# Single bias additions on GpSimd, wide conditioning products and a denser prologue in a two-layer conditioned attention kernel

## The chip, the cores and the metric

The kernel runs on one core of a Trainium2 chip. The metric is the device time of one execution in microseconds. TensorE (PE) does matrix products and transposes and writes to PSUM banks; VectorE (DVE), ScalarE (ACT) and GpSimd (POOL) work beside it; SyncE (SP) issues most DMA transfers from one queue, in order. Each engine runs its own instruction list in order and meets the others at semaphores.

## What is computed

Two attention layers, one behind the other, on x of shape (2, 1024, 256), float32, with a condition vector of 512 per batch element:

```
# layer 0: softmax attention, 16 heads of 16 channels
xn = layer_norm(x, norm_w, norm_b)
q, k, v = xn @ q_w + q_b, xn @ k_w + k_b, (xn @ v_w + v_b) * mask
att = softmax(q k^T + (1 - mask) * -1e6, over the keys)
y = att @ v
e = silu(emb) @ emb_w + emb_b              # (2, 512); scale, shift = its halves
h = layer_norm(y, sb_norm_w, sb_norm_b) * (1 + scale) + shift
x = x + silu(h) @ out_w + out_b
# layer 1: linear attention, 8 heads of 32 channels
q = softmax(xn @ Wq + bq, over channels); k = softmax(xn @ Wk + bk + mask term, over tokens)
v = (xn @ Wv + bv) * mask; y = q @ (k^T v); then as above with W_emb, b_emb, W_out, b_out
```

The condition's product e is small: 2 rows by 512 by 512 in each layer.

## The kernel before

Layer 0 is cut into 16 stages (`SUBS`): batch element x half of the queries (512) x group of 4 heads. A stage has 8 key tiles, so there are 128 steps (`STEPS`). In a step TensorE computes the scores of one key tile for four heads (`scores`, L969, four matmuls into the two double banks `sT`), ScalarE takes the exponential of both double banks (L803, `prob`), and in the next step TensorE multiplies with the values (`values`, L989, eight instructions into `acc`).

The softmax needs the largest score of each query before the exponential. So each stage has 32 "max" units (`MAXES`): TensorE computes scores with the queries as rows (L864) into one of three ring banks, VectorE reduces them (`halfmax`, L1162). The maxima of stage s+1 run beside the steps of stage s. Behind the last, VectorE makes `negmax` and splits it into two pieces (L1165, the cast L1168, L1170), TensorE transposes them (unit "neg", L882), VectorE copies them to `crows`, and SP loads them as rows of the queries (`load_max`). These small operations stand in VectorE's order behind maximum 32 and ahead of the maxima of the stage after.

All other work is cut into units placed beside the steps. A unit is filled by TensorE (`fill`) and taken out of its bank by ScalarE (if its kind is in `ON_ACT`) or VectorE:
- "rep" (L871, L875): queries and keys of group 0, replicated so that stage 0's maxima can start early.
- "qk" (L899): projection of queries and keys of one head group for 512 tokens; ScalarE writes its high part to `parts` (L735), VectorE the rest (L1203). `parts` has two buffers, group parity. `store_parts` writes them to HBM and `load_keys` and `load_queries` bring them back as stacked rows. Before ScalarE overwrites a buffer it waits for the stores of the group that held it.
- "v" (L839, L841): value projections of 256 tokens with a bias row `brow`; ScalarE writes `vp` (L746).
- "T" (L892): transposes of normalised rows `z`; "y", "neg", "kT", "qT": other transposes.
- "emb" (L913): e, as 4 x 4 products of a 128 x 128 weight block with two columns of the condition (`scond`), per layer; VectorE adds the bias (L1207), and behind the second computes the modulations.
- "out0", "keys", "queries", "values", "att", "y1", "out1": output projection of layer 0 and layer 1.

A planner writes `at[key]`, a spot of half a step, for each unit: `put` gives large kinds odd spots only, kinds in `SMALL` any. `places(k)` then says how many maxima stand at four places of step k (five where it has a large unit, three otherwise), and a rule on due times corrects the count. Before the steps runs a prologue: `pro_first`, then stage 0's 32 maxima with units of `between` among them (`pe_beside` is TensorE's order, `dve_beside` VectorE's), then `pro_last`. `warm` and `unread` issue matmuls of `ident` (L996) whose results nobody reads.

GpSimd normalises rows (`normalise`, L637 to L653) and adds output biases to `xs` (`add_bias`, L660): eight additions of 128 x 256 per batch element and layer. In layer 0 both elements' sixteen follow each other.

SP's list is: loads of inputs; `store_parts`, `load_keys`, `load_queries` of groups 1 and 2; the loads of `embw`, bias rows, `wo0` and `w1`; then per step the stores, loads and `load_max` that fall due.

Of the kernel before, what the change touches and what calls it, by code (L numbers as in the profile page):

```python
# [21 lines left out]
def two_layer_conditioned_attention(  # L22
# [59 lines left out]
    with ctx:  # L82
# [60 lines left out]
        def by_channel(flat):  # L143
            return flat.rearrange("p (k n) -> p k n", k=KC)
# [6 lines left out]
        qT = by_channel(late[:, 4 * TD:5 * TD])  # L151
        mrow = late[:, TD:TD + T]
# [53 lines left out]
        ON_ACT = {"T", "v", "values", "kT", "qT"}  # L206
# [5 lines left out]
        SMALL = {"T", "kT", "qT", "att", "vec2"}  # L212
# [33 lines left out]
        last = put([("qk", 0, 3, 0), ("qk", 0, 3, 1), ("qk", 0, 0, 1), ("v", 0, 3)], 0)  # L246
        last = put([("T", "in0", 1, h, kc) for h in range(NH) for kc in range(KC)], last)
        last = put([("emb", 0), ("emb", 1)], last)
        last = put([("qk", 1, hg, n) for hg in range(HG) for n in range(NH)], last)
# [109 lines left out]
        between = [("rep", *REPS[3]), ("qk", 0, 1, 0), ("rep", *REPS[4]), ("qk", 0, 1, 1), ("rep", *REPS[5])] + [("v", 0, i) for i in range(3)]  # L359
        pro_last = [("qk", 0, 2, n) for n in range(NH)]  # L360
        pe_beside, dve_beside = [], []
        for i in range(MAXES // 4):
            pe_beside += stream[4 * i:4 * i + 3] + [("warm", between[i], 1)] + stream[4 * i + 3:4 * i + 4] + [between[i]]
            behind = [between[i - 1]] if i > 0 and between[i - 1][0] != "v" else []
            dve_beside += stream[4 * i:4 * i + 2] + behind + stream[4 * i + 2:4 * i + 4]
        pe_beside += [("warm", pro_last[0], 2), ("neg", 0)] + pro_last
        dve_beside += [("neg", 0)] + pro_last
        pro_order = pro_first + between + pro_last
# [108 lines left out]
        def _(sp):  # L477
# [91 lines left out]
            for i, src in enumerate((emb_w, W_emb)):  # L569
                sp.dma_start(embw[:, i], src.rearrange("(e p) c -> p e c", p=P)).then_inc(embw_in, 16)  # L570
            for i, src in enumerate((out_b, b_out)):
                sp.dma_start(bias_rows[:, i, :], src.partition_broadcast(P)).then_inc(row_in, 16)
# [3 lines left out]
            for k in range(STEPS):  # L576
                for g in [3, 0] + list(range(HG, G)):
                    if k == begins["qk", g // HG, g % HG, 1] + 2:
                        store_parts(g)
                        if g == 3:  # L580
                            load_keys(g)
                s, c = where(k)
                if c == NT - 2 and s + 1 < SUBS:
                    load_max(sp, s + 1)
                if c == 0 and SLOTS <= s + 2 < SUBS:
                    load_queries(s + 2)
                if c == 0 and HG <= s - 1 < G:
                    load_keys(s - 1)
                if k == begins["emb", 1] + 2:
                    sp.wait_ge(emb_ready, 2)  # L590
                    load_mrow(0)
                if k == begins["att", 0, 1] + 2:
                    load_mrow(1)
                for half in range(2):
                    if k == begins["out1", 0, 2 * half + 1] + 2:
                        store(0, half)
# [5 lines left out]
        def _(pool):  # L602
# [52 lines left out]
            def add_bias(kind, b, row):  # L655

                for h in range(NH):
                    pool.wait_ge(z_ready[kind, b, h], QT)
                for t in range(b * NT, (b + 1) * NT):
                    pool.tensor_tensor(xs[:, t, :], xs[:, t, :], bias_rows[:, row, :], op=ALU.add).then_inc(biased, 1)  # L660
# [6 lines left out]

            for key in on_pool:
# [17 lines left out]
        def _(act):  # L686
# [11 lines left out]
            def take(key, ending=False):  # L698
# [44 lines left out]
                elif kind == "v":  # L743
# [4 lines left out]
                    last.then_inc(u.done, 1)  # L748
                elif kind == "values":
# [74 lines left out]
        def _(pe):  # L824
# [19 lines left out]
            def fill(key):  # L844
# [61 lines left out]
                elif kind == "emb":  # L906
                    l = key[1]
                    if l == 0:
                        pe.wait_ge(embw_in, 16 * 2)
                        pe.wait_ge(scond_ready, 1)  # L910
                    for oc in range(2 * KC):
                        for e in range(EC):
                            last = pe.matmul(o[:, oc * B:(oc + 1) * B], embw[:, l, e, oc * P:(oc + 1) * P], scond[:, :, e], start=(e == 0), stop=(e == EC - 1))  # L913
# [147 lines left out]
        def _(dve):  # L1061
# [61 lines left out]
            def take(key):  # L1123
# [81 lines left out]
                elif kind == "emb":  # L1205
                    l = key[1]
                    dve.scalar_tensor_tensor(out=emb[:, l], in0=o[:, 0:2 * KC * B].rearrange("p (o b) -> p o b", b=B), scalar=0.5, in1=by_col(f"emb_b{l}", 2 * KC),  # L1207
                                             op0=ALU.mult, op1=ALU.add).then_inc(u.done, 1)
# [77 lines left out]
            for key in pro_first:  # L1286
                if key[0] == "rep":
                    take(key)
            for key in dve_beside:
                take(key)  # L1290
                if key == ("max", 0, MAXES // 2):
                    dve.wait_ge(bhi_ready, 1)
                    dve.tensor_tensor(brow[32:33, :, :], braw[32:33, :, :], bhi[32:33, :, :], op=ALU.subtract).then_inc(brow_ready, 1)
# [30 lines left out]
```

## Time and profile before

| | us |
|---|---|
| median of three timed runs | 640.61 |
| lowest and highest of them | 638.69, 641.88 |
| the profiled execution | 630.65 |
| its span, first to last instruction | 628.7 |
| TensorE matmul busy | 580.3 (92%) |
| VectorE busy | 458.1 (73%) |
| ScalarE busy | 336.9 (54%) |
| GpSimd busy | 73.7 (12%) |

Matmuls overlap and their ends are modelled, so busy TensorE is not TensorE at its peak. The profile also records the clock granted to TensorE: 1.00 is 2.4 GHz, 0.50 is 1.2 GHz. Its mean over the span is 0.961. Times of rows count from the span's start.

### The profile page before, as it was taken

Reading aid. Unit: us, or ns where it says so; the run is one execution under the profiler, and the core shown is the slowest. Engines: PE = TensorE matmul, PEld = TensorE weight load, DVE = VectorE, ACT = ScalarE, POOL = GpSimd, SP = SyncE. Lnnn points to the kernel's source line nnn. Section 1 sums busy time; section 2 is a strip of 40 time slices with the busy share of each in tenths; the row PEclk is TensorE's granted clock in tenths of the full one; section 3 lists DMA queues with packets and bytes.
Section 4 is the critical chain, followed back from the end, with each engine's and each line's share of the span. In section 5 each row is a group of like instructions: output and inputs, shape, how many; then the busy total and the mean of one; then the engine's idle time right before and its main releaser. Section 6 shows DMA issues by size and latency. Waiting matters only on the chain.

```text
span 628.7 us, 8510 instructions
## 1 busy us (share of the span) xinstructions
PE 580.3 (92%) x3128; PEld 288.6 (46%) x3128; DVE 458.1 (73%) x916; ACT 336.9 (54%) x408; POOL 73.7 (12%) x125
## 2 busy tenths in 40 slices
PE   8999987999999999999998999999898999988986
PEld 7346335633453334344333434555334443524665
DVE  6585985378768899888889979868979897314543
ACT  2224461245558875646776655474574656771531
POOL 3000271000000040100002050000052001002200
PEclk9899996599999999999999979999989999999898
DMA  5245883127521003210330100010001100000001
GB/s 130 75 100 107 201 299 82 34 52 175 134 68 28 27 14 66 56 25 1 79 79 2 26 1 27 0 27 35 27 0 55 41 2 0 2 0 1 0 2 67
DMA packets 18579, 33.74 MB, mean 54 GB/s; under 512 B 3930, under 2 KB 10450, under 8 KB 17772
## 3 DMA queue, kind: packets, MB, share of 16 engines
q1 hardware_dynamic: 18412, 33.17, 21.2%
q8 instruction: 25, 0.41, 0.3%
q14 instruction: 14, 0.11, 0.1%
q10 hardware_dynamic: 128, 0.04, 0.0%
HBM read 19.29 MB, written 13.52 MB: 52 GB/s over the span
## 4 chain that ended last, share of the span: by engine, by line
PE 69%; DVE 22%; ACT 5%; issue 2%; DMA 1%; POOL 1%; SPq 0%; ACTq 0%; DVEq 0%; POOLq 0%
PE bank L989 16%; PE bank L864 13%; DVE halfmax L1162 12%; PE bank L839 8%; PE sT L969 7%; PE sT L839 3%; PE sT L864 3%; PE bank L899 3%; DVE stats L1076 2%; PE bank L913 2%; PE bank L925 2%; ACT hT L728 2%; ACT prob L803 2%; PE sT L871 2%; PE bank L996 2%
## 5 line engine op out<-in xcount | busy, mean ns | idle before, releaser
L803 ACT ACTIVATE prob<-sT 128x1024 f32<-128x1024 f32 x256 | 247.7, 1023 | 141.8 <-PE sT L969 141.5
L1162 DVE TENSOR_REDUCE halfmax<-bank 128x1 f32<-128x512 f32 x420 | 265.8, 683 | 54.6 <-PE bank L864 52.7
L864 PE MATMUL bank<-ks,qs 50*128 50x512 f32 x420 | 157.3, 483 | 17.4 <-DVE halfmax L1162 9.2
L989 PE MATMUL bank<-prob,vp 128*17 128x512 f32 x1024 | 139.7, 618 | 0.6 <-ACT prob L803 0.6
L864 PEld LDWEIGHTS bank<-ks,qs 50*128 50x128 f32 x420 | 64.5, 188 | 127.6 <-DVE halfmax L1162 76.1
L969 PE MATMUL sT<-qs,ks 52*128 52x512 f32 x512 | 108.2, 430 | 3.7 <-ACT prob L803 1.6
L637 POOL TENSOR_TENSOR rstd<-var,neghalf 128x4 f32<-128x4 f32 x14 | 14.2, 1015 | 532.1 <-DVE var L1086 532.1
L1162 DVE TENSOR_REDUCE halfmax<-sT 128x1 f32<-128x512 f32 x92 | 59.4, 685 | 11.6 <-PE sT L864 10.4
L969 PEld LDWEIGHTS sT<-qs,ks 52*128 52x128 f32 x512 | 54.8, 191 | 20.2 <-ACT prob L803 11.1
L839 PE MATMUL bank<-w,hT 128*128 128x256 f32 x152 | 38.7, 388 | 1.2 <-ACT hT L728 1.2
L989 PEld LDWEIGHTS bank<-prob,vp 128*17 128x17 f32 x1024 | 17.1, 96 | 40.6 <-issue 37.6
L839 PEld LDWEIGHTS bank<-w,hT 128*128 128x128 f32 x152 | 26.5, 189 | 9.0 <-issue 4.8
L864 PEld LDWEIGHTS sT<-ks,qs 50*128 50x128 f32 x92 | 8.8, 187 | 41.5 <-ACT prob L803 41.5
L864 PE MATMUL sT<-ks,qs 50*128 50x512 f32 x92 | 23.5, 508 | 0.5 <-ACT prob L803 0.5
L660 POOL TENSOR_TENSOR xs<-xs,bias_rows 128x256 f32<-128x256 f32 x32 | 22.0, 731 | 1.7 <-DVE z L1103 1.6
L899 PE MATMUL bank<-hT,wqk 128*128 128x512 f32 x44 | 21.6, 614 | 0.1
L735 ACT ACTIVATE late<-bank,cols 128x512 fp32r<-128x512 f32 x11 | 7.6, 689 | 26.2 <-PE bank L899 26.2
L892 PE MATMUL bank<-ident,z 128*128 128x128 f32 x96 | 14.7, 283 | 4.4 <-DVE z L1103 2.3
L1182 DVE RECIPROCAL rden<-bank 128x16 f32<-128x16 f32 x16 | 4.0, 251 | 20.1 <-PE bank L887 20.1
L841 PE MATMUL bank<-brow,ones 128*128 128x256 f32 x36 | 16.8, 468 | 0.0
L925 PE MATMUL bank<-hT,w 128*128 128x512 f32 x28 | 15.6, 682 | 1.1 <-ACT hT L728 1.1
L728 ACT ACTIVATE hT<-bank,modB,modA 128x512 f32<-128x512 f32 x12 | 9.1, 777 | 13.5 <-PE bank L892 13.1
(166 smaller groups left out, 559.1 us busy)
## 6 DMA issues: line engine op xcount, KB each, us to landing
stack_rows<-late SPq DMA_DIRECT2D x12, 512.0 KB, 6.0
qs<-stack_rows SPq DMA_DIRECT2D x30, 192.0 KB, 3.4
ks<-stack_rows SPq DMA_DIRECT2D x14, 384.0 KB
stack_rows<-late SPq DMA_DIRECT2D x17, 256.0 KB, 5.3
out_x<-xs SPq DMA_DIRECT2D x4, 512.0 KB, 3.0
xs<-in_x SPq DMA_DIRECT2D x4, 256.0 KB, 3.8
xs<-in_x SPq DMA_DIRECT2D x2, 512.0 KB, 4.2
late<-in_L_cond_emb_w SPq DMA_DIRECT2D x1, 1024.0 KB, 9.4
```

The costliest lines, as they stand in the source:

```text
L660: pool.tensor_tensor(xs[:, t, :], xs[:, t, :], bias_rows[:, row, :], op=ALU.add).then_inc(biased, 1)
L728: act.activation(hT[:, kc, h * HALF:(h + 1) * HALF], u.bank, func, scale=scale, bias=bias).then_inc(u.done, 1)
L803: act.activation(prob[:, c % 2, 2 * u:2 * u + 2, :].rearrange("p j n -> p (j n)"), sT[u][:, :], ACT.Exp).then_inc(exp_done, 1)
L839: last = pe.matmul(o[:, i * D:(i + 1) * D], hT[:, kc, tokens], w[:, kc, :], start=(kc == 0), stop=(kc == KC - 1 and row is None))
L841: last = pe.matmul(o[:, i * D:(i + 1) * D], ones[:, :], brow[:, row, :], start=False, stop=True)
L864: last = pe.matmul(o, qs[rows, s % SLOTS, c, t * P:(t + 1) * P], ks[rows, hg, c, half * HALF:(half + 1) * HALF], start=True, stop=True)
L892: last = pe.transpose(o[:, i * P:(i + 1) * P], z[:, h * QT + i, kc * P:(kc + 1) * P], ident[:, :])
L899: last = pe.matmul(o, wqk[:, kc, hg, :], hT[:, kc, n * HALF:(n + 1) * HALF], start=(kc == 0), stop=(kc == KC - 1))
L925: last = pe.matmul(o, w1[:, 1, k, kc * P:(kc + 1) * P], hT[:, k, n * HALF:(n + 1) * HALF], start=(k == 0), stop=(k == KC - 1))
L969: last = pe.matmul(sT[u][:, two * HALF:(two + 1) * HALF], ks[rows, hg, u, c * P:(c + 1) * P], qs[rows, s % SLOTS, u, :], start=True, stop= ...
L989: last = pe.matmul(acc[32 * j:32 * j + VW, :], vp[:, b, c, hg * GH + j, :], prob[:, c % 2, 2 * u + two, :], start=(c == 0), stop=(c == NT ...
L1162: dve.tensor_reduce(halfmax[:, s % 2, r, half:half + 1], o, axis=AX.X, op=ALU.max, negate=True).then_inc(u.done, 1)
```

## The change

Five edits:
1. `add_bias`: each addition on GpSimd first waits until the one before is complete.
2. "emb": the condition's two columns are the stationary operand and the 512 weight columns stream past, four products per layer into two rows of a bank. ScalarE copies them, halved, to `erow`. A new small unit "embT" transposes them by four 2 x 128 transposes, and VectorE adds the bias. "embT" stands behind the first two projections of batch element 1.
3. The prologue puts a unit behind every three maxima, without `warm` matmuls between, and has ten such units instead of eight: group 2's two projections have moved in among them. Each unit's part on VectorE comes after the second maximum of the next three.
4. Group 3's projections close the prologue (`pro_last`) instead of standing in steps 0 and 1; group 0's second projection and the last value unit move up from steps 2 and 3 to 0 and 1, and steps 2 and 3 have no unit. SP stores and loads group 3 behind the load of `embw`.
5. The subtraction for `brow` moves from VectorE to the head of GpSimd's list behind its fills.

```diff
-        ON_ACT = {"T", "v", "values", "kT", "qT"}
+        ON_ACT = {"T", "v", "values", "kT", "qT", "emb"}
-        SMALL = {"T", "kT", "qT", "att", "vec2"}
+        SMALL = {"T", "kT", "qT", "att", "embT", "vec2"}
-        last = put([("qk", 0, 3, 0), ("qk", 0, 3, 1), ("qk", 0, 0, 1), ("v", 0, 3)], 0)
-        last = put([("T", "in0", 1, h, kc) for h in range(NH) for kc in range(KC)], last)
+        last = put([("qk", 0, 0, 1), ("v", 0, 3)], 0)
+        last = put([("T", "in0", 1, h, kc) for h in range(NH) for kc in range(KC)], max(last, 4))
         last = put([("emb", 0), ("emb", 1)], last)
-        last = put([("qk", 1, hg, n) for hg in range(HG) for n in range(NH)], last)
+        last = put([("qk", 1, 0, n) for n in range(NH)], last)
+        last = put([("embT", 0), ("embT", 1)], last)
+        last = put([("qk", 1, hg, n) for hg in range(1, HG) for n in range(NH)], last)
...
-        between = [("rep", *REPS[3]), ("qk", 0, 1, 0), ("rep", *REPS[4]), ("qk", 0, 1, 1), ("rep", *REPS[5])] + [("v", 0, i) for i in range(3)]
-        pro_last = [("qk", 0, 2, n) for n in range(NH)]
+        between = [("rep", *REPS[3]), ("qk", 0, 1, 0), ("rep", *REPS[4]), ("qk", 0, 1, 1), ("rep", *REPS[5])] + [("v", 0, i) for i in range(2)]
+        between += [("qk", 0, 2, 0), ("v", 0, 2), ("qk", 0, 2, 1)]
+        pro_last = [("qk", 0, 3, n) for n in range(NH)]
         pe_beside, dve_beside = [], []
-        for i in range(MAXES // 4):
-            pe_beside += stream[4 * i:4 * i + 3] + [("warm", between[i], 1)] + stream[4 * i + 3:4 * i + 4] + [between[i]]
-            behind = [between[i - 1]] if i > 0 and between[i - 1][0] != "v" else []
-            dve_beside += stream[4 * i:4 * i + 2] + behind + stream[4 * i + 2:4 * i + 4]
+        by_three = [stream[i:min(i + 3, MAXES)] for i in range(0, MAXES, 3)]
+        for three, key, former in zip(by_three, between + [None], [("rep", *REPS[2])] + between):
+            pe_beside += three + ([key] if key is not None else [])
+            dve_beside += three[:2] + ([former] if former[0] != "v" else []) + three[2:]
...
                 sp.dma_start(embw[:, i], src.rearrange("(e p) c -> p e c", p=P)).then_inc(embw_in, 16)
+            store_parts(3)
+            load_keys(3)
...
                 for t in range(b * NT, (b + 1) * NT):
+                    pool.wait_ge(biased, t + row * B * NT)
                     pool.tensor_tensor(xs[:, t, :], xs[:, t, :], bias_rows[:, row, :], op=ALU.add).then_inc(biased, 1)
...
+            pool.wait_ge(bhi_ready, 1)
+            pool.wait_ge(zero_ready, 1)
+            pool.tensor_tensor(brow[32:33, :, :], braw[32:33, :, :], bhi[32:33, :, :], op=ALU.subtract).then_inc(brow_ready, 1)
...
+                elif kind == "emb":
+                    act.activation(erow[:, key[1], :], u.bank[0:B, :], ACT.Copy, scale=0.5).then_inc(u.done, 1)
...
+                    for e in range(EC):
+                        last = pe.matmul(o[0:B, :], scond[:, :, e], embw[:, l, e, :], start=(e == 0), stop=(e == EC - 1))
+                elif kind == "embT":
+                    l = key[1]
+                    done = unit["emb", l]
+                    pe.wait_ge(done.done, done.done_at)
                     for oc in range(2 * KC):
-                        for e in range(EC):
-                            last = pe.matmul(o[:, oc * B:(oc + 1) * B], embw[:, l, e, oc * P:(oc + 1) * P], scond[:, :, e], start=(e == 0), stop=(e == EC - 1))
+                        last = pe.transpose(o[:, oc * B:(oc + 1) * B], erow[:, l, oc * P:(oc + 1) * P], ident[0:B, 0:B])
```

## Rows read from the trace of the kernel before

**Rows 1.** The page: TensorE's granted clock in 40 slices, and the chain of waits.
```profile
PEclk9899996599999999999999979999989999999898
PE 69%; DVE 22%; ACT 5%; issue 2%; DMA 1%; POOL 1%; SPq 0%; ACTq 0%; DVEq 0%; POOLq 0%
```

**Rows 2.** Windows: stretch, its length, busy us (instructions) per engine, clock, DMA share, GB/s.
```profile
19.85:26.69 6.84, 5.60 (x12) 2.02 (x11) 3.14 (x5) 0.78 (x1) 0.00 (x0) 0.75 0.45 155
...
53.99:60.09 6.10, 5.94 (x32) 3.85 (x31) 1.78 (x3) 3.42 (x5) 0.00 (x0) 1.00 0.06 12
60.09:80.83 20.74, 18.64 (x86) 8.01 (x86) 18.57 (x40) 10.67 (x15) 3.42 (x6) 1.00 0.90 218
...
90.89:98.94 8.05, 2.55 (x18) 0.95 (x17) 8.02 (x5) 2.45 (x3) 6.45 (x10) 0.94 0.73 150
98.94:121.79 22.85, 22.85 (x100) 17.04 (x100) 7.33 (x13) 4.47 (x5) 0.00 (x0) 0.50 0.07 19
121.79:128.20 6.41, 6.41 (x28) 2.57 (x27) 4.69 (x16) 1.94 (x2) 0.00 (x0) 0.73 0.26 82
133.23:138.26 5.03, 4.73 (x24) 1.67 (x23) 3.92 (x6) 2.60 (x3) 0.00 (x0) 1.00 0.20 44
160.72:166.16 5.44, 5.14 (x28) 2.07 (x27) 4.51 (x8) 2.60 (x3) 0.00 (x0) 1.00 0.95 215
166.16:171.44 5.28, 4.97 (x30) 2.74 (x29) 3.92 (x6) 2.61 (x3) 0.00 (x0) 1.00 0.36 84
186.76:189.39 2.63, 2.60 (x19) 0.90 (x17) 2.12 (x4) 2.44 (x4) 0.00 (x0) 1.00 0.00 0
...
222.06:225.90 3.84, 3.26 (x19) 1.22 (x19) 3.60 (x10) 1.94 (x2) 3.02 (x6) 1.00 0.01 2
```

**Rows 3.** GpSimd and VectorE on the timeline; then cpieces' durations in ns (min/median/max).
```profile
86.33 11.01 POOL L660 TENSOR_TENSOR xs<-xs,bias_rows 128x256 f32<-128x256 f32 x16
90.65 6.72 DVE L1168 CAST cpieces<-negmax 128x16 fp32r<-128x16 f32 x1
...
L1168 DVE CAST cpieces<-negmax x16: 174/175/6720, 53.5 to 532.7; 128x16 fp32r<-128x16 f32 x16
```

**Rows 4.** TensorE on the timeline: value matmuls, idle time, an emb unit; weight loads.
```profile
91.88 1.05 PE L989 MATMUL bank<-prob,vp 128*17 128x512 f32 x8
98.24 0.40 PE L882 MATMUL bank<-ident,cpieces 128*32 128x128 f32 x1 [5.30 <-DVE halfmax L1162]
...
112.31 1.91 PE L989 MATMUL bank<-prob,vp 128*17 128x512 f32 x8
...
114.87 6.98 PE L913 MATMUL bank<-scond,late 128*128 128x2 f32 x32
...
7.74 2.98 PEld L996 LDWEIGHTS bank<-ident 128*128 128x128 f32 x26
```

**Rows 5.** The prologue on the timeline: TensorE between maxima, and four maxima on VectorE.
```profile
34.35 0.73 PE L864 MATMUL bank<-ks,qs 50*128 50x512 f32 x3
35.02 0.49 PE L996 MATMUL sT<-ident 128*128 128x128 f32 x2
36.06 1.98 PE L899 MATMUL sT<-hT,wqk 128*128 128x512 f32 x4
37.98 0.73 PE L864 MATMUL bank<-ks,qs 50*128 50x512 f32 x3
...
42.02 1.41 PE L864 MATMUL bank<-ks,qs 50*128 50x512 f32 x3
...
46.89 2.48 DVE L1162 TENSOR_REDUCE halfmax<-bank 128x1 f32<-128x512 f32 x4 [0.96 <-PE bank L864]
```

**Rows 6.** Timeline: VectorE's subtraction into brow; SP's first store and key load of group 2.
```profile
39.23 0.95 DVE L1293 TENSOR_TENSOR brow<-late 1x768 fp32r<-1x768 f32 x1
...
59.75 0.47 SPq L525 DMA_DIRECT2D stack_rows<-late  x1
...
68.58 0.78 SPq L534 DMA_DIRECT2D ks<-stack_rows  x2
```

More of the change, by code:

```diff
@@ L151, in two_layer_conditioned_attention @@
         qT = by_channel(late[:, 4 * TD:5 * TD])
+        erow = late[0:B, 4 * TD:4 * TD + 2 * E].rearrange("p (l c) -> p l c", l=2)
         mrow = late[:, TD:TD + T]
@@ L358, in two_layer_conditioned_attention @@
         pro_first += [("T", "in0", 0, 1, kc) for kc in range(KC)] + [("rep", *REPS[2])]
-        between = [("rep", *REPS[3]), ("qk", 0, 1, 0), ("rep", *REPS[4]), ("qk", 0, 1, 1), ("rep", *REPS[5])] + [("v", 0, i) for i in range(3)]
-        pro_last = [("qk", 0, 2, n) for n in range(NH)]
+        between = [("rep", *REPS[3]), ("qk", 0, 1, 0), ("rep", *REPS[4]), ("qk", 0, 1, 1), ("rep", *REPS[5])] + [("v", 0, i) for i in range(2)]
+        between += [("qk", 0, 2, 0), ("v", 0, 2), ("qk", 0, 2, 1)]
+        pro_last = [("qk", 0, 3, n) for n in range(NH)]
         pe_beside, dve_beside = [], []
-        for i in range(MAXES // 4):
-            pe_beside += stream[4 * i:4 * i + 3] + [("warm", between[i], 1)] + stream[4 * i + 3:4 * i + 4] + [between[i]]
-            behind = [between[i - 1]] if i > 0 and between[i - 1][0] != "v" else []
-            dve_beside += stream[4 * i:4 * i + 2] + behind + stream[4 * i + 2:4 * i + 4]
+        by_three = [stream[i:min(i + 3, MAXES)] for i in range(0, MAXES, 3)]
+        for three, key, former in zip(by_three, between + [None], [("rep", *REPS[2])] + between):
+            pe_beside += three + ([key] if key is not None else [])
+            dve_beside += three[:2] + ([former] if former[0] != "v" else []) + three[2:]
         pe_beside += [("warm", pro_last[0], 2), ("neg", 0)] + pro_last
         dve_beside += [("neg", 0)] + pro_last
+        assert len(by_three) == len(between) + 1
         pro_order = pro_first + between + pro_last
@@ L576, in _ @@
             for k in range(STEPS):
-                for g in [3, 0] + list(range(HG, G)):
+                for g in [0] + list(range(HG, G)):
                     if k == begins["qk", g // HG, g % HG, 1] + 2:
                         store_parts(g)
-                        if g == 3:
-                            load_keys(g)
                 s, c = where(k)
@@ L588, in _ @@
                     load_keys(s - 1)
-                if k == begins["emb", 1] + 2:
+                if k == begins["embT", 1] + 2:
                     sp.wait_ge(emb_ready, 2)
@@ L1204, in take @@
                                              op0=ALU.add, op1=ALU.subtract).then_inc(u.done, 1)
-                elif kind == "emb":
+                elif kind == "embT":
                     l = key[1]
-                    dve.scalar_tensor_tensor(out=emb[:, l], in0=o[:, 0:2 * KC * B].rearrange("p (o b) -> p o b", b=B), scalar=0.5, in1=by_col(f"emb_b{l}", 2 * KC),
-                                             op0=ALU.mult, op1=ALU.add).then_inc(u.done, 1)
+                    dve.tensor_tensor(emb[:, l], o[:, 0:2 * KC * B].rearrange("p (o b) -> p o b", b=B), by_col(f"emb_b{l}", 2 * KC), op=ALU.add).then_inc(u.done, 1)
                     dve.wait_ge(u.done, u.done_at)
@@ L1285, in _ @@
             dve.wait_ge(rep_cols_ready, 1)
-            for key in pro_first:
-                if key[0] == "rep":
-                    take(key)
+            for i in range(2):
+                take(("rep", *REPS[i]))
             for key in dve_beside:
                 take(key)
-                if key == ("max", 0, MAXES // 2):
-                    dve.wait_ge(bhi_ready, 1)
-                    dve.tensor_tensor(brow[32:33, :, :], braw[32:33, :, :], bhi[32:33, :, :], op=ALU.subtract).then_inc(brow_ready, 1)
             for k in range(STEPS + 2):
```

## Prediction

> **What bounds the kernel now.** I read the page first. The chain of waits is 69% TensorE and 22% VectorE, so the kernel lives on TensorE's sequence with VectorE close behind. The row of granted clocks has one deep notch, slices 7 and 8 of 40 (94 to 126 us), and a shallow one in slice 2 [rows 1]. The whole change lies ahead of 190 us, so I cut that stretch: TensorE's score matmuls (L969, four instructions per step) give the start of each of the 128 steps, and the view by windows, asked at those starts, gives one row per step or stage [rows 2]. The reader should compare steps that hold the same work. A step with one projection unit takes 5.03 us (the row 133.23:138.26), with a "y" unit beside it 5.44, with a value unit 5.28, a step with three maxima and a small unit 2.63. Against that step 6, also three maxima and a small unit, took 8.05, and steps 7 and 8, with the two "emb" units, took 22.85 together at clock 0.50. Step 9 took 6.41.
>
> What lies between is on the timeline [rows 3]. GpSimd runs 16 bias additions as one train from 86.33 to 97.34 us. VectorE's little cast (L1168) starts at 90.65 inside it and ends at 97.37, the moment the train ends: 6.72 us where the median of 16 is 175 ns. It is queued ahead of the maxima, which free the banks, so TensorE stands idle for 5.30 us. Right behind that the granted clock drops from 2.4 to 1.2 GHz: the same eight value matmuls take 1.91 us that elsewhere take 1.05, and an "emb" unit's 32 narrow products take 6.98 us [rows 4]. One collision thus pays twice.
>
> **The change part by part.** The sum is against the profiled execution: 628.7 us of span, 630.65 us in all, which is 10.0 us below the median of the three timed runs, 640.61.
>
> *Additions one by one.* Each of 32 additions waits for the former's completion. Nothing but later GpSimd work is queued behind them, and the first reader of a biased row is an output projection 35 steps later, so their lengthening is free. The cast then finds a gap, after at most one addition: a train of 11.01 us for 16 gives 0.69 each [rows 3]. Step 6 becomes 2.63 to 3.3 us; I take 2.8. Gain 5.2.
> The Trainium skill ("SBUF — State Buffer", section "SBUF: two separate sides") says that GpSimd and a two-port VectorE instruction take the shared port pair exclusively, for one whole instruction. By that rule the old cast should have lost one addition, 0.7 us; the trace disagrees, since it lost ten. Were the rule all there is, single additions would change nothing and the stall would need another cause; that is rival B.
>
> *Wide conditioning products.* Per layer 16 products of 2 columns (32 instructions) become 4 products of 512 columns, which at two instructions each, like L899's, are 8. Then comes one ScalarE copy and, later, four tiny transposes ("embT"). At full clock a projection of 4 such instructions costs 1.92 us (36.06 to 37.98) at about 0.43 each [rows 5], so 8 cost 3.64. The 32 narrow ones cannot be seen at full clock; nearest are the 26 weight loads of L996, 2.98 us, 0.115 each [rows 4], so 3.7. At equal clock the new form is worth nothing. At the clock of before it was 6.98. The bounds on what it is worth are therefore 0 and 2 x 3.3 us, and this depends on the clock. With TensorE no longer standing idle at 93 us I expect 2.4 GHz here, so steps 7 and 8 cost 5.03 + 1.72 = 6.75 each, 13.5 instead of 22.85: gain 9.35. Step 9, at full clock, is like step 17: 5.44 instead of 6.41, gain 1.0. ScalarE's copy falls into its idle time, since it is busy for only 2.60 us of a projection step's 5.03 [rows 2].
> "embT" makes a step of its own, step 11, and pushes ten later units one step back, to step 23, which was free. So the unit is not lost, but two small units are added: eight 0.115 us at most plus waits, 0.3 to 1.2 us; I take a loss of 0.6. VectorE's modulations move with it; they are needed only by "mid0", from step 34.
>
> *The prologue in threes.* Before, the first 32 maxima ran in eight fours, with a unit behind each four. From three maxima to the next three, a projection group took 3.63 (34.35 to 37.98), a replication group 4.04 (to 42.02), and in each of them 1.04 us (35.02 to 36.06) were the idle-filling matmuls (L996) and the fourth maximum, which waited for its bank [rows 5]. Now there are ten groups of three and a rest of two, without L996. By subtraction a group costs 2.59 and 3.00; one with a value unit 2.84, since a value step is 0.25 longer than a projection step [rows 2]. VectorE takes 0.62 per maximum (four in 2.48 [rows 5]) and for the unit about as much, 2.5 in all, so it hides, barely. The ten units are three replications, four projections and three values: 9.0 + 10.4 + 8.5 = 27.9 us. The first group starts at 19.85 as before, so the last unit ends at 47.7. Then the last two maxima must still be reduced (2 x 0.62) and followed by three small operations (0.2 each with their gaps), 2.0 us, which before ran beside the last value unit. From there the two final projections, L996 and step 0 follow as before, about 5.8 of the 6.10 us of the row 53.99:60.09: 55.5 us instead of 60.09 for the start of step 0, 4.6 earlier. The first group of before contained clock 0.75 on average and 1.24 us of waiting; whether that low stretch stays is open (0 to 1.5 us of loss), so I take a gain of 4.0, range 2.5 to 6. The subtraction into brow (0.95 us on VectorE [rows 6]) goes to GpSimd, idle then: 768 elements at 0.69 us per 256 are 2.1 us. By the group costs, ScalarE's two copies behind the third unit are done at about 30.5, GpSimd at 32.6, and the first value unit asks at 19.85 + 3 x 3.00 + 2 x 2.59 + 0.65 = 34.7: covered by 2 us.
>
> *The fourth group's projections ahead.* The two projections of group 3 leave steps 0 and 1. Steps 0 and 1 now hold what steps 2 and 3 held, and steps 2 and 3 hold no unit; the planner gives them 4 and 6 maxima. Step 36, five maxima and no unit, took 3.84, so I take 3.2 and 4.45. With 4.2 for step 0, which has no value matmuls but a small unit (5.03 - 1.05 + 0.2), and 5.28 for step 1 that is 17.1 instead of 20.74 [rows 2]: gain 3.6. The price on the queues: storing and loading of group 3 (four stores, two loads) now stand on SP's queue ahead of the bias rows, the output weights and layer 1's weights, whose first reader, GpSimd's additions, has slack. The additions may even start behind the cast now. Group 0's second projection comes at step 0 instead of 2, and ScalarE, before it writes its buffer, waits for group 2's stores. Those took from 59.75 until about 68.5 us [rows 6], 8.8 us, though issued only once group 2 is done. Now they would be issued at about 50.5 and land at 59.3; ScalarE asks at about 59.5. Cover nil, cost 0 to 1.5 us, in the range.
>
> Sum: 5.2 + 9.35 + 1.0 - 0.6 + 4.0 + 3.6 = 22.55 us, so 608.1 us for an execution like the profiled one and 618.1 if the 10.0 us to the median stay. Part of these 10 us can hardly be anything but longer stretches of low clock, and the largest such stretch goes away; I forecast 616.
>
> **Rivals.**
> A, *the clock falls elsewhere*. All the gain of steps 7 to 9 is clock. Steps 2 to 5 are now filled by VectorE's maxima (up to six per step), TensorE has gaps there, and idle TensorE is what preceded both notches. A stretch as long as the old one (steps 7 to 9, 29.3 us for what is worth 18.9) costs 10.4: 628.5. Against it: full clock held through steps 4 and 5, which have the same six maxima.
> B, *the train is not broken*. GpSimd takes the next addition so soon that the cast still waits for all, or the stall had another cause. Then step 6, the clock and steps 7 to 9 stay as before, wide products included, since 8 at half clock cost 7: gain 4.0 + 3.6 - 0.6 = 7.0, 633.6.
> C, *slower: the clock in the prologue*. The matmuls without use between the maxima are gone, and if the clock falls at 23 us, as it did before [rows 1, 2], it may not come back. TensorE's work from 19.85 to step 0 is some 30 us at full clock; at half it is up to 30 us more. Against a gain of 22.5 this decides from three quarters of the stretch at low clock: 640 to 648. Against it: groups with 2.5 of 2.6 us busy are busier than before.
> D, *a queue*. Group 2's stores land late and ScalarE holds up exponentials and maxima, or the first value unit waits for brow: 5 to 20 us, 621 to 638.
>
> **How the numbers follow.** Forecast 0.70, A 0.17, B 0.05, C 0.03, D 0.05. The likeliest case gives 616; its own spread is 603 (26 us gained and none of the 10 us left) to 624, and the range goes on through A to 630. A measurement can tell 0.5%, 3.2 us, from no change. Faster by more holds in the forecast, A, B and most of D, 0.94; within 0.5% the rest of D and a little of C, 0.03; slower 0.03.
>
> **What would show it.** Right: no cast above 1 us; no idle of TensorE above 1.5 us between 75 and 100 us; granted clock 1.0 in steps 6 to 9; the emb products 16 instructions at about 0.43 us from one to the next; step 0 at 54 to 57 us; steps 2 and 3 together under 8.5 us; step 10 starting 20 to 25 us earlier than 128.20. Wrong: a low clock of over 10 us anywhere ahead of 130 us (A or C), a cast of several us (B), ScalarE idle behind group 2's stores in step 0 (D).

## The result, and the profile after

The changed kernel takes 616.06 us (median of four runs, 610.35 to 622.21) where the kernel before takes 639.65 in the same comparison; the ratio is 0.965, 95% interval 0.959 to 0.971. The forecast was 616. The four runs lie in two pairs, 610.35 and 612.59 at mean clocks of 0.979 and 0.985, and 619.52 and 622.21, slow ones, at 0.958 and 0.960, so that no single run took 616. Measured again later beside the kernel before (e12) the ratio was 0.972, 0.967 to 0.976. The profiled execution took 610.35 us with a span of 608.5 us, 20.3 us less than the profiled one of before; the sum had said 22.55.

The page of the changed kernel, TensorE's share and its granted clock, beside [rows 1]:

```profile
PE 564.3 (93%) x3072; PEld 273.3 (45%) x3072; DVE 450.8 (74%) x915; ACT 337.9 (56%) x410; POOL 76.5 (13%) x126
...
PEclk9999899999999996999999999999899999999998
```

The notch in slices 7 and 8 is gone. A new narrow one (231 to 242 us) lies far behind the change, where the kernel before has one at 364 to 371 us, and a shallow one lies in slice 5.

The view by windows of the changed kernel at its own step starts (columns as in [rows 2]). In order: the ten groups of the prologue; from the last two maxima to step 0; steps 0 to 3; step 6; steps 7 and 8; step 9; steps 10 to 23.

```profile
19.92:48.47 28.55, 28.43 (x92) 13.77 (x91) 23.46 (x37) 9.26 (x15) 1.81 (x1) 1.00 0.56 132
48.47:58.44 9.97, 6.79 (x34) 4.25 (x33) 4.08 (x9) 3.24 (x4) 0.00 (x0) 1.00 0.57 131
58.44:77.93 19.49, 16.88 (x79) 7.51 (x80) 16.12 (x36) 9.35 (x12) 3.39 (x6) 0.91 0.94 252
88.41:90.60 2.19, 2.19 (x18) 0.83 (x17) 2.19 (x4) 2.05 (x3) 2.03 (x3) 1.00 1.11 357
90.60:102.77 12.17, 12.17 (x53) 3.12 (x52) 6.91 (x12) 5.33 (x7) 8.82 (x13) 1.00 0.21 61
102.77:107.65 4.88, 4.88 (x28) 2.05 (x27) 3.76 (x7) 2.53 (x3) 0.00 (x0) 1.00 0.00 0
107.65:171.16 63.51, 61.09 (x319) 26.63 (x320) 49.34 (x92) 35.51 (x44) 0.00 (x0) 1.00 0.50 121
```

Read against [rows 2]: step 6 took 8.05 and now 2.19; steps 7 and 8 took 22.85 at clock 0.50 and now 12.17 at 1.00; step 9 took 6.41 and now 4.88. These are 18.1 of the 20.6 us by which step 10 starts earlier (107.65 instead of 128.20). The prologue gave 1.65 (step 0 at 58.44 instead of 60.09) and steps 0 to 3 gave 1.25 (19.49 instead of 20.74). Steps 4 and 5 took 0.4 us more (10.48 instead of 10.06, each from the start of step 4 to that of step 6). Behind step 23 the changed kernel took 437.34 us where the kernel before took 436.48.

The timeline of the changed kernel shows the cast inside the now broken train, and the stretch ahead of step 0 where the forecast was off:

```profile
87.54 6.39 POOL L667 TENSOR_TENSOR xs<-xs,bias_rows 128x256 f32<-128x256 f32 x8 [3.15 <-DMA bias_rows<-in_L_cond_b_out]
88.15 0.17 DVE L1185 CAST cpieces<-negmax 128x16 fp32r<-128x16 f32 x1
...
51.63 0.47 SPq L530 DMA_DIRECT2D stack_rows<-late  x1
51.87 2.74 ACTq L471 DMA_DIRECT2D qs<-crows  x2
52.78 1.86 SPq L530 DMA_DIRECT2D stack_rows<-late  x1
54.75 1.95 PE L1013 MATMUL bank<-ident 128*128 128x128 f32 x16
58.41 0.72 PE L986 MATMUL sT<-qs,ks 52*128 52x512 f32 x4 [1.71 <-DMA qs<-crows]
```

An addition now comes every 0.80 us (8 in 6.39) instead of 0.69. The load of the row maxima (ACTq L471) takes 2.74 us to issue while SP issues group 2's stores (e7 shows that they are the cause), and TensorE then waits 1.71 us for it.

### The profile page after: what moved, and what is told of

It reads as the page before. It is cut to its first block and busy times, and to the rows that moved or that the text cites. A ratio compares the mean times of both kernels' runs of the same rounds, so it can differ in the third digit from the quotient of the medians.

```text
span 608.5 us, 8404 instructions
## 1 busy us (share of the span) xinstructions
PE 564.3 (93%) x3072; PEld 273.3 (45%) x3072; DVE 450.8 (74%) x915; ACT 337.9 (56%) x410; POOL 76.5 (13%) x126
## 5 line engine op out<-in xcount | busy, mean ns | idle before, releaser
L876 PE MATMUL bank<-ks,qs 50*128 50x512 f32 x424 | 154.3, 481 | 16.0 <-DVE halfmax L1179 8.5
L1006 PE MATMUL bank<-prob,vp 128*17 128x512 f32 x1024 | 136.8, 606 | 0.6 <-ACT prob L815 0.6
L986 PE MATMUL sT<-qs,ks 52*128 52x512 f32 x512 | 106.6, 426 | 4.9 <-DMA qs<-crows 2.5
L1179 DVE TENSOR_REDUCE halfmax<-sT 128x1 f32<-128x512 f32 x88 | 56.8, 685 | 8.0 <-PE sT L876 6.9
L667 POOL TENSOR_TENSOR xs<-xs,bias_rows 128x256 f32<-128x256 f32 x32 | 23.3, 728 | 7.2 <-DMA bias_rows<-in_L_cond_b_out 3.2
L876 PE MATMUL sT<-ks,qs 50*128 50x512 f32 x88 | 22.0, 495 | 0.4 <-ACT prob L815 0.4
L911 PE MATMUL bank<-hT,wqk 128*128 128x512 f32 x36 | 19.3, 662 | 0.2 <-DVE halfmax L1179 0.2
L1199 DVE RECIPROCAL rden<-bank 128x16 f32<-128x16 f32 x16 | 4.0, 251 | 19.9 <-PE bank L899 19.9
L745 ACT ACTIVATE late<-bank,cols 128x512 fp32r<-128x512 f32 x9 | 6.2, 687 | 21.4 <-PE bank L911 21.4
L738 ACT ACTIVATE hT<-bank,cols 128x512 f32<-128x512 f32 x12 | 8.9, 774 | 14.8 <-PE bank L904 14.6
L738 ACT ACTIVATE hT<-bank,modB,modA 128x512 f32<-128x512 f32 x12 | 9.1, 776 | 13.6 <-PE bank L904 13.2
```

The costliest lines, as they stand in the source:

```text
L738: act.activation(hT[:, kc, h * HALF:(h + 1) * HALF], u.bank, func, scale=scale, bias=bias).then_inc(u.done, 1)
L876: last = pe.matmul(o, qs[rows, s % SLOTS, c, t * P:(t + 1) * P], ks[rows, hg, c, half * HALF:(half + 1) * HALF], start=True, stop=True)
L911: last = pe.matmul(o, wqk[:, kc, hg, :], hT[:, kc, n * HALF:(n + 1) * HALF], start=(kc == 0), stop=(kc == KC - 1))
L986: last = pe.matmul(sT[u][:, two * HALF:(two + 1) * HALF], ks[rows, hg, u, c * P:(c + 1) * P], qs[rows, s % SLOTS, u, :], start=True, stop= ...
L1006: last = pe.matmul(acc[32 * j:32 * j + VW, :], vp[:, b, c, hg * GH + j, :], prob[:, c % 2, 2 * u + two, :], start=(c == 0), stop=(c == NT ...
L1179: dve.tensor_reduce(halfmax[:, s % 2, r, half:half + 1], o, axis=AX.X, op=ALU.max, negate=True).then_inc(u.done, 1)
```

## Experiments

All ratios are to the kernel before, measured on the same chip in turn. The changed kernel itself ran beside none of e1 to e8; what is said of them against it goes by the ratios or by single profiles.

### Edit 1 alone, and the train cut in other ways

```diff
 # e1_single, on the kernel before
                 for t in range(b * NT, (b + 1) * NT):
+                    pool.wait_ge(biased, t + row * B * NT)
                     pool.tensor_tensor(xs...)
 # e2_fours:         the wait only if t % 4 == 0
 # e9_eights:        the wait only if t % 8 == 0
 # e10_two_fourteen: the wait only if t + row * B * NT == 2
```

> The kernel before with edit 1 alone (each bias addition waits for the one before). Theory P (one collision pays twice: the stall of the cast, then the clock that TensorE's idle time brings down): the cast behind stage 1's maxima takes under 1 us, step 6 takes about 2.8 us instead of 8.05, and with TensorE never idle there the clock stays at 2.4 GHz, so that steps 7 and 8, still with narrow products, take 6.7 to 7.0 us each instead of 11.4. In all 15 us less, ratio to before about 0.976. Rival N (the narrow products themselves bring the clock down): the cast is short as well, but the granted clock falls to 0.5 in step 7 or 8, steps 7 to 9 keep some 25 to 29 us, and only about 5 us are gained, ratio 0.992.

Measured: 0.982 (0.976 to 0.987), 623.03 us. The windows of steps 6, 7 and 8:

```profile
93.53:95.73 2.20, 2.20 (x17) 0.84 (x17) 2.17 (x5) 2.06 (x3) 1.87 (x4) 1.00 0.34 78
95.73:102.91 7.18, 7.18 (x51) 5.55 (x50) 3.60 (x7) 2.34 (x3) 5.65 (x8) 0.85 0.85 201
102.91:114.38 11.47, 11.47 (x51) 8.50 (x50) 3.44 (x6) 2.54 (x3) 0.00 (x0) 0.50 0.01 1
```

The stall is gone, TensorE is busy throughout, and yet the clock falls within step 7, in the first unit of narrow products, and step 8 takes 11.47 us as before. The cast took 0.47 us. So the stall is not needed for the low clock: that part of theory P falls, and rival N's mechanism is seen. The time lies between the two.

> The kernel before with the wait ahead of every fourth bias addition only, so the train of 16 becomes four trains of 4, about 2.7 us each. Theory P (a train without a gap holds the cast until its end): the cast starts in the seventh addition and ends with the eighth, so it takes 1 to 2 us; in general at most 2.8. Rival R (the pair of ports is handed over after each instruction, and the 6.72 us had another cause): the cast takes either under 0.8 us or again about 6.7 us. Time by theory P: step 6 about 1 us longer than with single additions, clock held, ratio to before about 0.978.

Measured: 0.980 (0.972 to 0.989). The cast took 0.70 us, not 1 to 2. It was asked for in the third addition of its four and let in ahead of the fourth, which no wait kept back. Theory P, as I had put it for a train without a gap, is wrong, and the cast is as short as rival R had it. Two more cuts place it:

> The kernel before with one wait in the bias additions, ahead of the ninth: two trains of 8. The cast should be asked for within the seventh addition, as before. Theory S (a gapless train lets VectorE in while it is young and holds it to its end once it has run for some additions: in earlier runs the cast was let in when asked for in the third addition of its train, and lost everything when asked for in the seventh): the cast waits until the eighth addition ends, 1.0 to 1.4 us. Rival (it is let in between two additions here too): under 0.75 us. Rival (waits for all sixteen again): 6 to 7 us.

> The kernel before with one wait in the bias additions, ahead of the third: a train of 2 and one of 14. The cast is asked for at about the fifth addition of the train of 14, with nine more behind it. Theory S with the point of change between the third and the seventh addition leaves both open here, and the run places it: under 0.8 us if at the fifth VectorE is still let in, 6 to 7 us if the train already holds it. The theory that only the number of additions behind the cast counts (nine, as before) expects 6 to 7 us.

GpSimd's train and VectorE's cast on the timelines of e9 and then of e10:

```profile
90.78 5.54 POOL L662 TENSOR_TENSOR xs<-xs,bias_rows 128x256 f32<-128x256 f32 x8
95.11 1.24 DVE L1170 CAST cpieces<-negmax 128x16 fp32r<-128x16 f32 x1
```

```profile
86.36 11.16 POOL L662 TENSOR_TENSOR xs<-xs,bias_rows 128x256 f32<-128x256 f32 x16
90.69 0.68 DVE L1170 CAST cpieces<-negmax 128x16 fp32r<-128x16 f32 x1
```

Each ran once (621.58 and 624.06 us), so only their traces are used. In e9 the cast is asked for at 95.11, in the seventh addition (additions come every 0.69 us from 90.78), and passes over the change to the eighth; it ends when the train of 8 ends. In e10 the merged row hides the one wait: the train of 14 starts at 87.87, and the cast comes at 90.69 in its fifth addition. Nine more follow, just as in the kernel before, and it loses 0.5 us. So the number of additions behind the cast does not decide. What goes with the loss, in all six traces, is how long the train has run without a wait. With e5 below:

| kernel | train | cast asked for in its | additions behind it | cast, us |
|---|---|---|---|---|
| e5 | 16 | 3rd | 13 | 0.57 |
| e2 | 4 | 3rd | 1 | 0.70 |
| e10 | 14 | 5th | 9 | 0.68 |
| before | 16 | 7th | 9 | 6.72 |
| e3 | 16 | 7th | 9 | 6.71 |
| e9 | 8 | 7th | 1 | 1.24 |

The third position was seen twice, the fifth once, the seventh three times, the sixth never. What changes between the fifth and the seventh was not found.

### Edit 2 alone, and all but edit 2

```diff
 # e3_wide, on the kernel before: edit 2 as in the change (emb, embT, erow), nothing else
 # e4_narrow, on the changed kernel: edit 2 undone, all else as changed
```

> The kernel before with edit 2 alone (wide conditioning products with their copy and small transposes); the train of additions stays. Theory P: the cast again takes 6 to 7 us, the clock falls to 0.5 right behind it as before. What the wide products then cost depends on how long it stays low: if it stays for both, steps 7 and 8 take about 11.4 us each as before (8 instructions at 0.86 us) and the time is the same, ratio 0.997 to 1.003. Rival W (wide products are work that brings the clock back, narrow ones are not): the low stretch is 3 to 10 us instead of 27.3, steps 7 to 9 take 20 to 24 us instead of 29.3, 5 to 9 us less, ratio 0.986 to 0.992.

Measured: 0.982 (0.974 to 0.990). The cast took 6.71 us again, as did step 6 its 8.04, but steps 7 to 9 took 19.9 us instead of 29.3. Windows of steps 7 and 8 of e3:

```profile
98.95:107.81 8.86, 8.86 (x27) 2.33 (x27) 3.90 (x7) 1.94 (x2) 0.00 (x0) 0.65 0.17 47
107.81:113.92 6.11, 6.11 (x28) 1.59 (x27) 3.18 (x5) 3.02 (x4) 0.00 (x0) 1.00 0.00 0
```

Rival W holds, more strongly than I had priced it: the low stretch is 10.2 us long (95.0 to 105.2) instead of 27.3, the clock comes back within the first wide unit (103.41 to 107.87) and stays. In the kernel before it stayed low through both narrow units and 3.4 us beyond, until 125.2. With the stall whole, edit 2 alone is worth as much as edit 1 alone.

> The changed kernel with edit 2 undone (narrow conditioning products, no small transposes); all else as changed. Theory P: without the stall the clock stays at 1.0 in steps 7 to 9, and at full clock 32 narrow instructions cost what 8 wide ones do, so steps 7 and 8 take 6.1 to 6.4 us each as in the changed kernel and the whole time is within 1 us of it, ratio to before about 0.964. Rival N: the clock falls to 0.5 in step 7 or 8 and some 5 to 10 us come back, ratio 0.972 to 0.98.

Measured: 0.980 (0.969 to 0.991), against 0.965 and 0.972 for the changed kernel. By the ratios edit 2 gives 5 to 10 us on top of the others, but the intervals touch or overlap. The two profiles differ by 7.7 us of span (616.2 and 608.5), 4.6 of them in steps 7 and 8. The windows of these steps in e4, its two units of narrow products on the timeline, and then the first wide unit of the changed kernel:

```profile
90.99:97.20 6.21, 6.21 (x52) 4.57 (x51) 3.66 (x7) 2.35 (x3) 5.57 (x8) 1.00 0.26 70
97.20:107.72 10.52, 10.52 (x52) 7.99 (x51) 3.35 (x6) 2.54 (x3) 2.30 (x4) 0.56 0.01 2
...
93.53 3.73 PE L920 MATMUL bank<-scond,late 128*128 128x2 f32 x32
100.80 6.99 PE L920 MATMUL bank<-scond,late 128*128 128x2 f32 x32
```

```profile
93.11 3.60 PE L924 MATMUL bank<-late,scond 128*2 128x512 f32 x8
```

Here both theories are half right, and the run shows why. Step 7 ran its 32 narrow products wholly at full clock: 3.73 us for the unit against 3.60 for the wide one, 6.21 us against 6.07 for the step. At equal clock the form is worth 0.1 us. But the clock falls in every profile that has narrow products without the stall: within the first unit in e1, e2, e5, e9 and e10, and 1.2 us behind the first unit in e4. In e2, e9 and e10 it rises between the two units and falls again within the second. In none of the seven profiles with wide products did a low stretch begin within them. What it is in the narrow products that the clock answers to was not found.

### Edits 3, 4 and 5 alone

```diff
 # e5_three_edits: the changed kernel with edits 1 and 2 undone
```

> The changed kernel with edits 1 and 2 undone, so edits 3, 4 and 5 alone (prologue in threes, the fourth group's projections ahead, brow on GpSimd). Theory P (a train without a gap holds the cast until its end): the train begins at about 86.8 us and the cast is asked for at about 88.6, so it now waits for some 13 more additions, 9 to 9.5 us, longer than before; step 6 takes 10 to 11 us, the clock falls behind it, and steps 7 and 8 take about 11.4 us each. The whole then stands at the time of before less what prologue and steps 0 to 3 gained (about 2.2 us by the changed kernel's trace) plus 2.5: ratio 0.995 to 1.005. Rival R (a handover after an addition or two is possible without a gap, as the train of fours let it in between its third and its fourth): cast under 1.5 us, and only the narrow products' low clock remains: ratio about 0.98.

Measured: median 628.49 us over four runs that spread from 617.0 to 634.8, beside 631.13. The whole train of 16 and the cast, and the windows of steps 7 and 8:

```profile
87.45 11.03 POOL L663 TENSOR_TENSOR xs<-xs,bias_rows 128x256 f32<-128x256 f32 x16 [2.19 <-DMA bias_rows<-in_L_cond_b_out]
89.01 0.57 DVE L1174 CAST cpieces<-negmax 128x16 fp32r<-128x16 f32 x1
...
91.63:99.53 7.90, 7.90 (x50) 6.42 (x51) 3.81 (x7) 2.15 (x3) 6.85 (x10) 0.77 0.20 54
99.53:111.01 11.48, 11.48 (x52) 8.51 (x51) 3.44 (x6) 2.54 (x3) 0.00 (x0) 0.50 0.00 1
```

I had expected 9 us and found 0.57. The bias rows land late here (the wait of 2.19 us), so the train starts 1.1 us later than in the kernel before, and the cast comes 1.6 us earlier. The train is young when the cast comes, and it is let in without any wait of edit 1. In the changed kernel the train starts even later against the cast (87.54 and 88.15). So edits 3 to 5 remove the stall in this profile without edit 1. That it is edit 4's delay of the bias rows' load that does it is argued, not shown, and so is that the changed kernel could do without edit 1: neither was run apart.

### Ahead of step 0

```diff
 # e7_late_store, on the changed kernel
             load_queries(1)
+            sp.wait_ge(cmax_in, 32)
             store_parts(2)
 # e6_halves: store_parts(2, range(NH)) instead, the counts of parts_stored to match
 # e8_fill: unread(free.bank, 15) instead of 8
```

> The changed kernel with group 2's stores held back until the row maxima of stage 0 have landed. Theory Q: the issue on ScalarE's queue takes about 1.4 us again, the rows land at about 55, and step 0 starts at about 56.8, when the idle-filling matmuls and VectorE's last part are done; but the stores land only at about 63, so ScalarE waits 1 to 3 us for its buffer in step 0 and the net is a gain or a loss of at most 1.5 us. Rival: step 0 is not earlier than 58.4, the rows' landing has another cause.

Measured: 0.977 (0.970 to 0.985). The issue on ScalarE's queue, step 0, and ScalarE's wait behind it:

```profile
51.91 1.42 ACTq L471 DMA_DIRECT2D qs<-crows  x2
57.02 0.72 PE L987 MATMUL sT<-qs,ks 52*128 52x512 f32 x4 [0.32 <-issue]
63.44 0.69 ACT L746 ACTIVATE late<-bank,cols 128x512 fp32r<-128x512 f32 x1 [3.94 <-DMA stack_rows<-late]
```

Theory Q holds in what it says of the load: without SP's stores beside it the issue takes 1.42 instead of 2.74 us and step 0 starts at 57.02, 1.4 us earlier; step 0 takes 4.23 us, since TensorE no longer stood idle. ScalarE then waits 3.94 us for group 2's stores and step 1 takes 7.54 instead of 6.38, which is rival D's mechanism at the size that the forecast had bounded (0 to 1.5 us). Step 2 starts 1.9 us earlier (68.79 instead of 70.69). The stores themselves were not held up by the load, as theory Q also had it: SP's four issues took 0.47, 0.60, 1.86 and 1.21 us in both kernels. The time is no better all the same; in this profile the clock is low for 17.1 us, from 81.4 to 98.5 (see e8).

> The changed kernel with group 2's stores issued in two halves, the first when its first projection is done (about 44 us), the second as before at about 51.6. Theory Q (in the changed kernel the load of the row maxima, issued on ScalarE's queue at 51.87, and group 2's stores, issued on SP's at 51.63, hold each other up: the issue takes 2.74 us instead of 1.43 and the rows land at 58.4): with half the bytes at 51.6 the issue takes 1.4 to 2.2 us, step 0 starts at 56.5 to 57.5 instead of 58.4, TensorE's idle time ahead of it is under 1 us and the clock stays up: 2 to 4 us less than the changed kernel. Rival: the issue is as slow with small stores, step 0 stays at 58.4 and the time is the same.

Measured: median 618.10 us (604.41 to 619.50) beside 631.13, not told apart from the changed kernel. The issue took 1.60 us, as expected, but step 0 gained nothing in the profile: the clock was low from 55.8 to 59.2 us and the last two projections took 5.37 us instead of 3.67. Its lowest run, 604.41 us at a mean clock of 0.990, is the fastest of all runs here. Inconclusive.

> The changed kernel with 15 instead of 8 idle-filling matmuls ahead of step 0, so that TensorE works through the 1.7 us that it waits for the row maxima. They delay nothing before 58.4 us. Theory K (idle TensorE ahead of step 0 brings the clock down from 60.7 to 64.1): the low stretch goes away, step 0 takes 4.2 to 4.6 us instead of 5.88, 1.3 to 2 us less in all. Rival: the clock falls in the first steps all the same (their gaps suffice) and the time is the same or a little longer.

Measured: 0.981 (0.975 to 0.987). Windows of steps 0 and 1, and of steps 4 and 5:

```profile
62.50:66.73 4.23, 3.63 (x16) 1.66 (x16) 3.22 (x7) 1.94 (x2) 0.00 (x0) 1.00 0.56 132
66.73:73.20 6.47, 5.57 (x32) 3.02 (x31) 5.78 (x11) 3.54 (x6) 0.00 (x0) 1.00 1.03 188
...
80.43:88.26 7.83, 7.41 (x28) 3.52 (x28) 4.92 (x15) 3.49 (x4) 3.39 (x6) 0.50 0.73 159
88.26:95.63 7.37, 7.01 (x26) 3.62 (x28) 4.14 (x9) 3.20 (x4) 4.39 (x6) 0.50 0.95 268
```

Step 0 takes 4.23 us instead of 5.88: with TensorE kept busy the low stretch at 61 us is gone, as theory K had it. In the four profiles whose clock falls at 60.7 to 61.8 us for 3.4 us (changed kernel, e4, e5, e12) TensorE had waited 1.7 to 2.3 us for the row maxima; in e7 and e8 TensorE waited 0.32 us or less, and there is no such stretch. But a longer one, 17.1 us, appears at steps 4 to 6, and costs about 5 us (steps 4 and 5 take 15.20 us instead of 10.48). It is there in e6 and e7 too (from 79.7 and 81.4 us), and in none of the four profiles just named. This is rival A's mechanism. Whether it comes in part of the executions whatever the kernel, or because the short low stretch at 61 us is missing, one profile of each can't tell.

### Against the low clock in steps 4 and 5

```diff
 # e11_spread, on the changed kernel, with e7's wait
-        last = put([("qk", 0, 0, 1), ("v", 0, 3)], 0)
+        put([("qk", 0, 0, 1)], 1)
+        last = put([("v", 0, 3)], 3)
 # e12_again: the changed kernel unaltered
```

> The changed kernel with group 0's second projection in step 1 and the last value unit in step 3 (steps 0 and 2 hold no unit instead of 2 and 3), and group 2's stores held back until stage 0's row maxima have landed. Theory L (in the changed kernel steps 2 to 5 have no projection, TensorE's work with full columns thins out, and in part of the executions the clock falls to 0.5 from about 80 us for 17 us, which costs 5 to 8 us): with the value unit in step 3 that low stretch is seen more rarely or not at all, step 0 starts 1.4 us earlier, ScalarE's wait for the stores is covered by one more step, and the median is 3 to 8 us below that of the changed kernel run beside it. Rival: the low stretch comes with step 4's and 5's six maxima whatever stands ahead; the two medians then differ by less than 2 us.

> The changed kernel once more, unaltered, beside the run with spread units on the same chip. Theory L: its times lie in two groups, about 609 to 612 us where the clock holds through steps 4 and 5, and 616 to 622 us where it falls there; the mean granted clock of each run goes with its time (0.98 against 0.96). Rival (the spread of times has another cause than the clock): runs with the same clock differ by over 5 us.

Measured: e11 0.975 (0.970 to 0.981), 621.14 us; e12 0.972 (0.967 to 0.976), 616.36 us. Spreading the units is no better. The windows of steps 1, 3 and 5 of e11:

```profile
66.72:75.04 8.32, 7.54 (x24) 2.62 (x25) 5.43 (x11) 2.72 (x4) 0.00 (x0) 0.64 0.78 143
...
77.28:84.46 7.18, 5.74 (x32) 2.83 (x28) 6.30 (x19) 3.15 (x5) 3.41 (x6) 1.00 1.06 395
...
89.82:96.04 6.22, 5.67 (x27) 2.40 (x27) 3.72 (x8) 2.87 (x4) 2.18 (x4) 0.73 1.06 269
```

The low stretch has moved to step 1, behind a step 0 that now holds no unit (TensorE busy 2.20 of its 4.19 us), step 0 starts no earlier than before (38.8 us behind the first maximum, as against 38.5 in the changed kernel), and step 3 with the value unit takes 7.18 us at full clock. Theory L falls as a recipe. Of e12's six runs those at mean clock 0.979 and 0.985 took 611.55 and 613.14, those at 0.959 to 0.966 took 617.0 to 621.6, and the one at 0.976 took 615.69, so the two groups are not as clean as I had them. The spread of times goes with the clock, to within about 2 us. Where in the kernel the longer ones lose it no trace shows, since the profiled run was the shortest (span 609.2 us, clock 1.00 in steps 1 to 23).

## Why the prediction was right, point by point

**Step 6** (gain 5.2 forecast, 5.86 measured): right. The cast took 0.17 us, less than one addition. But the reason given, a gap made by edit 1, is only one of two that suffice; e5 has no such gap, its train starts late, and the cast took 0.57. The profile before held one observation of a stalled cast, and I made a law of the whole train out of it.

**Steps 7 and 8** (gain 9.35 forecast, 10.68 measured): right in size, half wrong in cause. I wrote that at equal clock the new form is worth nothing, which e4 shows (6.21 against 6.07), and that TensorE no longer standing idle would hold the clock. e1 refutes the second: without the idle time the narrow products themselves let the clock fall. Removing the stall and turning the products were both needed, and rival B's price was wrong for the same reason. I gave the wide products no gain behind a stall, and e3 gained 1.8% with the stall whole.

**Step 9** gave 1.53 against 1.0 forecast. **"embT"**, forecast as a loss of 0.6, cost nothing that can be seen: steps 10 to 23 took 63.51 us, where 128.20 to 192.22 of before is 64.02.

**The prologue** (gain 4.0 forecast, 1.65 measured): the group costs were right, 28.55 us for ten groups against 27.9. The step that failed is "from there the two final projections, L996 and step 0 follow as before". It took 9.97 us from the last two maxima to step 0, where I had 7.8. Of these 2.2 us more, 1.42 are the row maxima's load, which e7 gives back. The 8.50 left in e7 are 5.77 from the two projections to step 0, as forecast, and 2.73 ahead of them, where I had 2.0. I had put group 2's stores at 50.5 us for ScalarE's sake and had not asked what else issues a transfer then: the row maxima's load. In the kernel before these were 4.6 us apart (55.11, and 59.75 [rows 6]) and its issue took 1.43 us, as this row of its timeline has it:

```profile
55.11 1.43 ACTq L466 DMA_DIRECT2D qs<-crows  x2
```

**Steps 0 to 3** (gain 3.6 forecast, 1.25 measured): two terms mis-sized. Step 1 took 6.37 us, for which I took 5.28 from a value step of batch element 1. The same unit in step 3 of before had taken 6.35; I had that step only inside the merged row 60.09:80.83. And step 0 took 5.88 instead of 4.2, because TensorE's wait of 1.71 us for the row maxima was followed by 3.4 us of low clock; e7 and e8 have 4.23. Steps 2 and 3 were 7.24 against 7.65 forecast. Windows of the kernel before (its step 3) and of the changed one (behind the wait):

```profile
74.48:80.83 6.35, 5.55 (x31) 3.00 (x30) 5.66 (x11) 3.44 (x5) 2.24 (x5) 1.00 1.05 320
```

```profile
60.00:64.20 4.20, 4.02 (x7) 1.45 (x7) 3.32 (x8) 0.88 (x1) 0.00 (x0) 0.59 0.68 117
```

**Brow on GpSimd** (forecast 2.1 us, covered): it took 1.81 and no value unit waited. **Step 0's buffer** (cost 0 to 1.5): none in the changed kernel, 1.2 us in e7, where the stores are later.

**The signs.** Of those named, one was missed: step 0 started at 58.44, not at 54 to 57. Step 10 started 20.55 us earlier, at the lower end of what was named.

**The median.** The profiled run came out 2.2 us above its sum, the median on the forecast. That the median is met to 0.1 us is luck: steps 6 to 9 gave 2.5 us more than forecast, prologue and steps 0 to 3 gave 4.7 less, and no single run took 616. The 10.0 us between profile and median of before were guessed to be low clock. The kernel before, run again beside e1 to e12, bears it out: 25 runs from 625.97 us at a mean clock of 0.971 to 640.84 at 0.938. In the changed kernel the distance is 5.7 us and e12's runs show it to be mostly that. Rival A's stretch is in neither profile of the changed kernel, but in those of e6, e7 and e8; whether its runs at a mean clock of 0.96 have it is open. Rival C did not happen, though the first 15 us, which the change does not touch, show the same kind of effect (below).

## What to carry to other kernels

Price a matrix product by what it does to TensorE's clock as well as by its own time: here many loads with two streamed columns cost the same at full clock as few long streams (3.73 and 3.60 us), and then brought 13.6 to 20.5 us of low clock. When a transfer is moved, list every transfer that any queue issues at its new time, the small urgent ones above all. Where a stall is explained by one row, run that row at another position before making it a rule.

## What the runs showed of the hardware

The cast on VectorE, 128 x 16, was let in between two of GpSimd's additions when asked for in the third or fifth of a train without waits (0.57 to 0.70 us, three kernels), and held to the train's end when asked for in the seventh (6.72, 6.71 and 1.24 us). The Trainium skill ("SBUF — State Buffer", section "SBUF: two separate sides") says that of two instructions that need the shared pair of ports, the one that starts first gets it for the whole instruction and the other blocks. A wait of at most one addition agrees with that; the held casts, which waited through two to ten of them, need something more, which no run here shows.

The issue of two loads of 8 KB on ScalarE's queue took 2.74 us beside SP's issue of 512 and 256 KB stores and 1.42 us alone, in the same kernel but for one wait (e7). SP's own issues took the same in both, so the cost fell on one side only.

The pace of TensorE in the first 15 us differs between executions of the same instructions. The 26 idle-filling matmuls at the start, in the changed kernel and in e8:

```profile
7.75 3.17 PE L1013 MATMUL bank<-ident 128*128 128x128 f32 x26
```

```profile
9.15 5.92 PE L1013 MATMUL bank<-ident 128*128 128x128 f32 x26
```

They start 1.4 us later, since twelve small products ahead of them took 2.72 instead of 1.49 us, and take 1.9 times as long, so that the first maximum starts at 24.0 us instead of 19.9. That is the pace of 1.2 instead of 2.4 GHz for nearly all of the row, by the durations alone: the profile of e8 has no record of the clock ahead of 15.1 us. Three of the fourteen profiles (e6, e8, e11) lost some 4 us so, two others (e1, e2) 2.6 us. The 4 us are more than the 2.9 that prologue and steps 0 to 3 gained.
